# Keys and values made by rows from x in two parts, queries moved behind the context, w1 and w2 staged in SBUF

## The reference

```python
Q = x @ wq.T;  K = x @ wk.T;  V = x @ wv.T               # 4096 x 64 each
energy  = einsum('nd,ne->de', K, V)                      # 64 x 64
context = Q @ energy * sqrt(3 / 64)
x = layernorm(x + context @ wo.T)
h = silu((x @ w1.T) * s1) * ((x @ w2.T) * s2)            # 4096 x 1024
h = gelu((h @ h1.T) * s_h1);  h = gelu((h @ h2.T) * s_h2)
out = layernorm(x + (h @ w3.T) * s3)
```

## Time and profile before

| | us |
|---|---|
| median of 3 runs (lowest, highest) | 647.01 (646.89, 647.16) |
| the profiled execution | 647.28 |
| its span, first to last instruction | 645.5 |
| PE busy | 635.5 (98%) |
| DVE busy | 491.1 (76%) |
| ACT busy | 411.0 (64%) |
| POOL busy | 280.6 (43%) |

### The profile page before, as it was taken

One profiled execution on the slowest core, in us unless ns is written; L12 is line 12 of the kernel. 1 busy time (PEld: TensorE's weight loads), 2 busy tenths in 40 slices (PEclk: granted clock), 3 DMA queues, 4 the chain that ended last, 5 costly groups with the idle time before them and its releaser, 6 DMA issues.

```text
span 645.5 us, 9171 instructions
## 1 busy us (share of the span) xinstructions
PE 635.5 (98%) x3147; PEld 531.1 (82%) x3148; DVE 491.1 (76%) x722; ACT 411.0 (64%) x697; POOL 280.6 (43%) x225
## 2 busy tenths in 40 slices
PE   8989999999999999999999999999999999999996
PEld 6768887888789888888889888888889888888896
DVE  5687799989565996789665898698754899488477
ACT  6579688868672566558661757656763466666655
POOL 0376999492001762096000564078000367069025
PEclk9999999999999999999999999999999999999999
DMA  8999889953310056434330036734330015534301
GB/s 342 391 367 401 321 333 354 378 205 130 133 67 0 2 163 229 162 131 147 129 116 1 1 97 191 251 118 159 130 131 1 0 20 188 184 131 144 118 1 67
DMA packets 24370, 103.89 MB, mean 161 GB/s; under 512 B 2224, under 2 KB 3312, under 8 KB 16496
## 3 DMA queue, kind: packets, MB, share of 16 engines
q1 hardware_dynamic: 24032, 102.98, 45.1%
q10 hardware_dynamic: 288, 0.26, 0.1%
HBM read 87.51 MB, written 23.07 MB: 171 GB/s over the span
## 4 chain that ended last, share of the span: by engine, by line
PE 97%; DVE 1%; issue 0%; POOL 0%; POOLq 0%; ACT 0%; DVEq 0%
PE ps L1395 63%; PE ps L1338 18%; PE ps L1464 8%; PE ps L1487 1%; PE ps L1270 1%; PE ps L1204 1%; PE ps L1232 1%; PE ps L1258 1%; PE ps L1246 1%; PE ps L1220 1%; PE ps L1252 0%; PE ps L1239 0%; DVE st L1125 0%; DVE xr L1132 0%; POOL rstd L512 0%
## 5 line engine op out<-in xcount | busy, mean ns | idle before, releaser
L1395 PE MATMUL ps<-R,ring 128*128 128x512 f32 x1792 | 410.2, 390 | 0.2 <-issue 0.2
L1395 PEld LDWEIGHTS ps<-R,ring 128*128 128x128 f32 x1792 | 335.2, 188 | 69.9 <-issue 0.6
L984 DVE TENSOR_TENSOR R<-quarter,R 128x512 fp32r<-128x512 f32 x284 | 262.0, 946 | 58.8 <-ACT R L709 58.5
L709 ACT CAST R<-quarter 128x512 fp32r<-128x512 f32 x284 | 173.2, 616 | 30.0 <-POOL quarter L540 12.0
L1338 PE MATMUL ps<-x1T,w 128*128 128x512 f32 x512 | 119.1, 391 | 0.6 <-issue 0.5
L755 ACT ACTIVATE quarter<-U,sc 128x512 f32<-128x512 f32 x96 | 69.5, 724 | 73.7 <-DVE U L1011 28.3
L1338 PEld LDWEIGHTS ps<-x1T,w 128*128 128x128 f32 x512 | 95.4, 188 | 21.9 <-ACT quarter L755 0.9
L530 POOL TENSOR_TENSOR quarter<-quarter,quarter 128x512 f32<-128x512 f32 x32 | 50.4, 1576 | 95.0 <-ACT quarter L755 88.3
L673 ACT ACTIVATE sg<-ps,sc 128x512 f32<-128x512 f32 x64 | 44.2, 690 | 63.6 <-PE ps L1338 63.5
L481 POOL TENSOR_TENSOR ve<-mv,eps 128x4 f32<-128x4 f32 x14 | 5.6, 403 | 180.4 <-DVE mv L961 180.4
L725 ACT COPY U<-ps 128x512 f32<-128x512 f32 x96 | 56.2, 585 | 28.7 <-PE ps L1395 28.5
(11 more groups left out here) (97 smaller groups left out, 389.1 us busy)
## 6 DMA issues: line engine op xcount, KB each, us to landing
ring<-combos SPq DMA_DIRECT2D x56, 1024.0 KB, 4.9
combos<-unit SPq DMA_DIRECT2D x8, 1024.0 KB, 8.5
unit<-in_h1T SPq DMA_DIRECT2D x4, 1024.0 KB, 14.6
xr<-in_x_rows SPq DMA_DIRECT2D x8, 512.0 KB, 5.1
unit<-in_h2T SPq DMA_DIRECT2D x4, 1024.0 KB, 8.7
xT<-in_xT SPq DMA_DIRECT2D x7, 512.0 KB, 7.7
out<-xr SPq DMA_DIRECT2D x7, 512.0 KB, 3.0
w<-w_dram SPq DMA_DIRECT2D x3, 1024.0 KB, 9.3
```

What stands on the lines that cost most here:

```text
L709: nc.scalar.copy(R[slot_of(p, u)][:, 0, c, :], quarter[operand_home(p, u)][:, c, :]).then_inc(hi_done, 1)
L984: nc.vector.tensor_tensor(r[:, 1, c, :], quarter[operand_home(p, u)][:, c, :], r[:, 0, c, :].bitcast(f32), ALU.subtract).then_inc(lo_done, 1)
L1395: last = nc.tensor.matmul(ps[:, bank + j, :], w, view(R[slot_of(p, u)][:, part, k, :]), start=n in (0, 1, 5) and k == 0 and part == 0, sto ...
```

## The change

- Keys and values of blocks 2 to 7 are made by rows from the two parts: `kv_of_parts` has, for each of 4 tiles, 4 fp32r matmuls with a 128x128 piece of `xhi` or `xlo` stationary and `wkvr` (128 columns) moving. The transposed products, the turning and their copies go. VectorE copies blocks 0 to 2, ScalarE 3 to 7, into four buffers in place of two.
- All eight blocks keep their own `xhi` (the last four where the ring is loaded later), so rounding waits for no queries. The low part of block 1 moves from VectorE to the head of GpSimd's queue.
- Queries: only block 0's stand ahead of keys and values. Of block 1, two pieces stand ahead of T1; the other 26 stand behind it. The 5 warm-up products go; the banks change.
- ScalarE's order changes: `bits_of_w12(0)` ahead of T1's rounding, `bits_of_whole(1)` behind `hi_of_transposed(0, 6)`, `bits_of_whole(2)` and `(3)` at j = 2 and 3 of the first silu loop, in place of j = 0 and 5, with the sums of unit 0 at j = 0 and 1.
- w1 and w2 are loaded into SBUF where units 3 and 4 come later (`w12_stage`), looked at there and copied within SBUF. Loads of units 3 and 4 wait for that. `load_unit(4)` is issued behind the stores of the queries, `load_ring(5)` ahead of `load_rows_late`.

The diff, cut to its core:

```diff
--- before.py
+++ after.py
@@ -49,13 +49,11 @@
-Q_BETWEEN = 4
+KV_DVE = 3
...
-Q_BANK = (4, 5, 6, 7, 5, 4, 5, 3)
+Q_BANK = (4, 5, 6, 7, 4, 6, 7, 4)
...
-WARM_MIDDLE = 5
@@ -152,10 +151,11 @@
-        kvT = [over(f"kvT{i}", q_at + 8192 + 1024 + 2048 * i, [P, BLK]) for i in range(2)]
...
-        xhi = [over(f"xhi{i}", x1T_at + 4096 * i, [P, EC, BLK], f32r) for i in range(4)]
+        xhi = [over(f"xhi{f}", x1T_at + 4096 * f if f < 4 else ring_at + 4096 * (f - 4), [P, EC, BLK], f32r) for f in range(NB)]
...
+        w12_stage = over("w12_stage", u_at, [P, 2 * EC * HID])
@@ -310,14 +310,14 @@
-            def relay_w12(i):
+            def stage_w12(i):
                 at = i * EC * HID
-                sp.dma_start(w12_dram[:, at:at + EC * HID], (w1_in, w2_in)[i]).then_inc(w12_relayed[i], 16)
+                sp.dma_start(w12_stage[:, at:at + EC * HID], (w1_in, w2_in)[i]).then_inc(w12_staged[i], 16)
...
                 at = i * EC * HID
-                sp.wait_ge(w12_relayed[i], 16)
-                sp.dma_start(w12[:, at:at + EC * HID].bitcast(f32), w12_dram[:, at:at + EC * HID]).then_inc(w12_in[i], 16)
+                sp.wait_ge(w12_staged[i], 16)
+                sp.dma_start(w12[:, at:at + EC * HID].bitcast(f32), w12_stage[:, at:at + EC * HID]).then_inc(w12_in[i], 16)
@@ -327,6 +327,9 @@
                     sp.wait_ge(l1_tile, 2 * HC * (i - 5))
+                if 3 <= i <= 4:
+                    sp.wait_ge(w12_in[i - 3], 16)
+                    sp.wait_ge(bits_done, n_bits("w12", i - 3))
                 src = sources[i // KH].rearrange("p (h i n) -> p h i n", h=2, i=KH)[:, :, i % KH, :]
@@ -371,16 +374,16 @@
             store_unit(0)
+            relay_hidden(0, 0)
             store_q(4)
-            relay_hidden(0, 0)
-            load_unit(4)
-            store_unit(1)
             store_q(5)
...
             store_q(7)
-            store_unit(2)
+            load_unit(4)
+            store_unit(1)
             load_ring(0)
             relay_hidden(0, 1)
+            store_unit(2)
             store_unit(3)
@@ -391,10 +394,10 @@
             relay_hidden(1, 0)
+            load_ring(5)
             load_rows_late(3)
...
             relay_hidden(1, 1)
-            load_ring(5)
             store_unit(5)
@@ -551,6 +554,10 @@
+            pool.wait_ge(kv_ready, 2)
+            pool.wait_ge(xhi_done, 2)
+            nc.gpsimd.tensor_tensor(tiles_of(xlo[1]), tiles_of(xT[1]), xhi[1].bitcast(f32).rearrange("p c (t n) -> p c t n", t=TPB),
+                                    ALU.subtract).then_inc(second_xlo, 1)
@@ -596,10 +603,12 @@
-            def copy_kvt(f):
...
-                act.wait_ge(kvt_ready, f - 1)
-                nc.scalar.copy(kvT[f % 2][:, :], ps[:, KV_BANK[f], :]).then_inc(kvt_out, 1)
+            def copy_kv(f):
...
+                act.wait_ge(kv_ready, f + 1)
+                if f >= 4:
+                    act.wait_ge(et_ready, f - 3)
+                nc.scalar.copy(kv[f % 4][:, :], ps[:, KV_BANK[f], :]).then_inc(later_kv_out, 1)
@@ -608,13 +617,11 @@
-                if f >= 4:
-                    act.wait_ge(q_ready, f - 3)
-                nc.scalar.copy(xhi[f % 4].rearrange("p c (t n) -> p c t n", t=TPB), tiles_of(xT[f])).then_inc(xhi_done, 1)
+                nc.scalar.copy(xhi[f].rearrange("p c (t n) -> p c t n", t=TPB), tiles_of(xT[f])).then_inc(xhi_done, 1)
...
-                act.wait_ge(w12_in[i], 16)
-                bits(low_halves(w12[:, i * EC * HID:(i + 1) * EC * HID]), 0, i)
+                act.wait_ge(w12_staged[i], 16)
+                bits(low_halves(w12_stage[:, i * EC * HID:(i + 1) * EC * HID]), 0, i)
@@ -826,44 +833,42 @@
                 high_x(f)
-            copy_kvt(2)
             hi_of_q(0)
             high_x(5)
-            copy_kvt(3)
-            hi_of_q(1)
             high_x(6)
-            copy_kvt(4)
-            raw_q(2)
+            copy_kv(3)
             high_x(7)
-            raw_q(3)
-            for f in range(5, NB):
-                copy_kvt(f)
+            copy_kv(4)
+            copy_kv(5)
             bits_of_whole(0)
-            raw_q(4)
+            copy_kv(6)
+            copy_kv(7)
+            bits_of_w12(0)
             act.wait_ge(t1_ready, 1)
             nc.scalar.activation(T1s[:, 0, :], ps[:, 3, 0:E], ACT.Copy, scale=CTX_SCALE).then_inc(t1_hi, 1)
-            for i in range(2):
-                bits_of_w12(i)
-            bits_of_whole(1)
+            hi_of_q(1)
+            bits_of_w12(1)
+            raw_q(2)
+            raw_q(3)
+            raw_q(4)
             for q in range(ACT_TILES[0]):
...
             raw_q(6)
+            raw_q(7)
             hi_of_transposed(0, 6)
-            raw_q(7)
+            bits_of_whole(1)
             act.wait_ge(cst_in, 16 * NCST)
...
                 silu(0, j, A)
-                if j == 0:
-                    bits_of_whole(2)
+                if j <= 1:
+                    bits_of_sums(0, range(j, j + 1))
                 if 2 <= j <= 3:
-                    bits_of_sums(0, range(j - 2, j - 1))
+                    bits_of_whole(j)
                 if j == TR1_AFTER:
...
                     hi(0, 0, j - KH)
-                if j == 5:
-                    bits_of_whole(3)
             for j in range(HC):
@@ -1091,24 +1096,22 @@
             nc.vector.memset(zeros[:, :], 0.0).then_inc(zeros_made, 1)
-            for f in range(NB):
+            def copy_kv(f):
                 dve.wait_ge(kv_ready, f + 1)
-                if f >= 2:
-                    dve.wait_ge(et_ready, f - 1)
-                nc.vector.tensor_copy(kv[f % 2][:, :], ps[:, KV_BANK[f], :]).then_inc(kv_out, 1)
-                if f == 0:
-                    low_x(0)
-                    flag_out(0)
-                elif f == 1:
-                    low_x(2)
-                    low_x(1)
-                    low_x(3)
-                    low_x(4)
-                    lo_of_q(0)
-                elif f <= 4:
-                    if f == 4:
-                        lo_of_q(1)
-                    low_x(f + 3)
+                nc.vector.tensor_copy(kv[f][:, :], ps[:, KV_BANK[f], :]).then_inc(kv_out, 1)
+
+            copy_kv(0)
+            low_x(0)
+            flag_out(0)
+            copy_kv(1)
+            low_x(2)
+            low_x(3)
+            low_x(4)
+            copy_kv(2)
+            lo_of_q(0)
+            low_x(5)
+            low_x(6)
+            low_x(7)
             dve.wait_ge(et_ready, NB)
@@ -1144,6 +1147,7 @@
+            lo_of_q(1)
@@ -1197,10 +1201,10 @@
-                            pe.wait_ge(*((qlo_done, 2), (qlo_done, 1), (q_raw, 3), (tile_sum[0], TPB))[b - 4])
+                            pe.wait_ge(*((qlo_done, 1), (q_raw, 1), (q_raw, 2), (q_raw, 3))[b - 4])
...
-                        pe.wait_ge(xlo_done, n_xlo(b))
-                    x = xhi[b % 4][:, c, :] if part == 0 else tiles_of(xlo[b])[:, c, :, :]
+                        pe.wait_ge(*((second_xlo, 1) if b == 1 else (xlo_done, n_xlo(b))))
+                    x = xhi[b][:, c, :] if part == 0 else tiles_of(xlo[b])[:, c, :, :]
@@ -1221,28 +1225,27 @@
-            def kv_transposed(f, view):
...
-                if f > 2:
-                    pe.wait_ge(kv_out, f - 2)
-                for part in range(2):
-                    pe.wait_ge(*((xhi_done, f + 1) if part == 0 else (xlo_done, n_xlo(f))))
-                    for c in range(EC):
-                        x = xhi[f % 4][:, c, :] if part == 0 else tiles_of(xlo[f])[:, c, :, :]
-                        last = nc.tensor.matmul(ps[:, KV_BANK[f], :], wkvr[:, c, :] if view is exact else wkv[:, c, :], view(x),
-                                                start=part == 0 and c == 0, stop=part == 1 and c == 1)
-                last.then_inc(kvt_ready, 1)
...
-            def kv_turned(f):
-                pe.wait_ge(kvt_out, f - 1)
+            def kv_of_parts(f, view):
...
+                if f >= 3:
+                    pe.wait_ge(*kv_copied(f - 3))
+                pe.wait_ge(xhi_done, f + 1)
+                pe.wait_ge(xlo_done, n_xlo(f))
...
-                    last = nc.tensor.transpose(ps[:, KV_BANK[f], q * P:(q + 1) * P], kvT[f % 2][:, q * P:(q + 1) * P], ident[:, :])
+                    for part in range(2):
+                        for c in range(EC):
+                            x = xhi[f][:, c, q * P:(q + 1) * P] if part == 0 else tiles_of(xlo[f])[:, c, q, :]
+                            last = nc.tensor.matmul(ps[:, KV_BANK[f], q * P:(q + 1) * P], view(x), wkvr[:, c, :] if view is exact else wkv[:, c, :],
+                                                    start=part == 0 and c == 0, stop=part == 1 and c == 1)
...
+            def kv_copied(f):
+                return (kv_out, f + 1) if f < KV_DVE else (later_kv_out, f - KV_DVE + 1)
...
-                pe.wait_ge(kv_out, f + 1)
+                pe.wait_ge(*kv_copied(f))
...
-                    k, v = kv[f % 2][:, q * P:q * P + D], kv[f % 2][:, q * P + D:(q + 1) * P]
```

(57 more changed lines are left out.)

3 lines of the change are left out of this document (removed).

## The result

The changed kernel is slower. In the first round the median over both groups was 657.7 against 647.05 before; the lower group stands to the kernel before as 1.0075 (95% interval 1.0056 to 1.0095), in the second round as 1.0068 (1.0053 to 1.0082).

The account below looks back on a forecast made before the run. TensorE was taken to bound the kernel, with 97% of the last-ending chain. The terms -0.7 - 0.1 + 3.1 - 0.2 = +2.1 us took the profiled 647.28 to 649.4, median 649.1; range 645.7 to 651.8.

Parts of the forecast that it names:

- The sum: Whole kernel: all terms together +2.1 us, so 649.4 for the profiled execution and 649.1 for the median.
- Part 1: TensorE's stretch ahead of product T1: 16.8 us against 17.45, so T1 starts 0.7 us earlier.
- c: Spacing of fp32r matmuls of 128 columns ahead of T1: taken as 0.115 us, within 0.107 to 0.128.
- The engines that feed this stretch keep up: Ahead of T1: VectorE, ScalarE and GpSimd deliver in time despite moved work; cost taken as 0.
- Part 2: From T1 to the first w1 product: 14 more query pieces are hidden, change -0.1 us.
- Rival (c), the clock: Wait at block 1's transposes: TensorE's clock falls there, adding 1.6 to 2.5 us; chance 12%.
- Part 3: Block 1's transposes: its deviation, queued on GpSimd behind combinations that start later, makes TensorE wait 3.1 us.
- Part 4: Transfers: copying w1 and w2 within SBUF and later unit loads cost 0; an earlier ring load gives -0.2 us.
- The hole at ring 5: TensorE's hole of 0.21 us ahead of 106.66: issuing `load_ring(5)` earlier removes it, -0.2 us.

Follow-up runs that it names:

- e1: Changed kernel with block 1's low part moved from GpSimd back to VectorE; median 650.62 us, ratio 1.0054.
- e3: Changed kernel with block 1's low part back on VectorE and block 1's deviation ahead of unit 2 in GpSimd's queue; median 646.13 us, ratio 0.9973.
- e10: e7 with 12 wide warm-up products put between the narrow ones; 650.78 to 653.75 us, ratio 1.0092.
- b5: Kernel before with only block 1's low part moved to the head of GpSimd's queue; median 649.21 us, ratio 1.0025.
- b6: Kernel before with only ScalarE's looks put in the new order; median 652.26 us, ratio 1.0077.
- e4: Changed kernel with six warm-up products filling the hole ahead of the first narrow products; median 651.88 us, ratio 1.0078.
- e2: Changed kernel with block 1's deviation ahead of unit 2 in GpSimd's queue; seven executions 646.45 to 648.38 us (ratio 0.9997), three 657.5 to 658.6.
- e7: e3 with its first narrow products made to wait for VectorE's low part of block 4; 647.68, 658.05, 658.65 and 658.96 us.
- b8: Kernel before with its first 128x512 products of keys and values made to wait for block 4's low part; median 653.17 us, ratio 1.0091.
- a0: Changed kernel measured again, unedited, in a second round; four executions 649.38 to 652.77 us, two 662.95 and 664.15.

## Why the prediction was wrong

- **The sum** came out for one execution in eleven, the one whose clock holds: +2.1 forecast, a span of 647.5 against 645.5, and 649.38 against the 649.4 I had put on the profiled execution. In part this is luck, as the next point shows.
- **Part 1.** The stretch from energy(1) to T1 took 16.82 in that execution (10.99 to 27.81), as my 16.8, but by two errors that cancel. Without the hole it takes 15.93 (e1, e3), 0.9 less than I had: the six blocks 11.3 against 11.84 and the seven energies 4.0 against 4.27. The hole of 0.84, which I had put at nothing, made up for it. T1 was 1.0 earlier and not 0.7 because that execution also came to this place earlier (block 0's query pieces began at 9.91, before at 10.29).
- **c** was 0.112 us (14 steps of two products between the starts 14.19 and 17.32 in e10), against my 0.115. Of the two rules of the Trainium skill's "TensorE: Matmul & The Clock Gate" that I had weighed, LDWEIGHTS with 107 ns is near this, and Back-to-back issue gap with 81 ns is not.
- **"The engines that feed this stretch keep up"** is the first step that failed, a wait that I put at nothing. I gave GpSimd the low part of block 1 as free because GpSimd was idle, and did not ask what runs on VectorE beside it. It stretched VectorE's low part of block 2 from 1.2 to 2.9 us and opened a hole of 0.84 in one trace and 1.37 in the other. I had even used the same effect in part 2, to explain 2.19 against 1.38. The Trainium skill ("SBUF — State Buffer", Who interferes with whom) says that a VectorE instruction with two SBUF inputs and a GpSimd instruction that reads SBUF lock each other out. e1 and b5 agree with it: VectorE's three low parts took 3.49 without GpSimd's subtraction beside them and 5.24 with it.
- **Rival (c), the clock**, is the second, and the larger. I looked for a fall only in the wait at block 1, gave it 12%, and priced it at 1.6 to 2.5. It was seen there in three of five traces that have the wait (the upper group's, e1, b6; not in the lower group's nor e4) and cost 1.4 to 1.6. And I did not put it at the front at all, where it costs 11: that is how far the medians of the two groups lie apart in the changed kernel, in e2 and in e7. What I had not asked is how the clock comes back. Behind the hole it fell, and under the narrow products it stayed down for some 20 us (the upper group's trace and e7), while b8 had it back after 3.4. Which property of the narrow stream does that (its 128 columns, a weight load for every product) was not tested.
- **Part 2:** from T1 to the first w1 product 9.99, before 9.87: +0.1 instead of -0.1. The 14 more pieces are hidden, as forecast.
- **Part 3** held step by step. After T1's start: `combine(1)` at +11.37 (forecast +11.3), unit 2's first addition at +17.19 (+17.2), the deviation at +19.82 (+19.8), VectorE's tiles at +21.16 (+21.15), the wait 2.93 (3.1). b6 shows that the order of ScalarE's looks alone makes it, e2 that GpSimd's order alone removes it.
- **Part 4:** the copies within SBUF took 6.2 us each, not 9.3, and were hidden as before. The hole at ring 5 went, but by 157 us holes of 0.24 behind a flag's sum and 0.17 ahead of transposes had taken its place, so -0.2 was 0.

## What to carry to other kernels

Before giving work to an idle engine, ask what the other engines that read SBUF do at that moment, and which waits on others stand behind it in the same queue: one subtraction here held up TensorE, and two tiny operations behind six large ones cost 2.9 us. Don't put a long run of narrow matmuls behind a place where TensorE may stand still. If it must be, fill the place (e4) or put wide products between (e10); each had four executions and no long one. A sum that meets the measured time is not yet right: here a hole and too high a price for the products hid each other. And work that can move behind the point where another engine sets the pace is worth moving (3.2 us of queries were hidden), while the form of the products ahead of it has to be priced by itself.

## What the runs showed of the hardware

- fp32r matmuls with 128 moving columns and a new weight each start 0.112 us apart at 2.4 GHz and 0.2135 at 1.2 GHz; with 512 columns it is 0.23 at 2.4 GHz. So a narrow one does a quarter of the columns in half the time.
- Under such a stream, with single energies of 64 columns between, a fallen clock stayed at 0.50 for 19.6 us (the upper group's trace) and 21.4 us (e7) without a hole. In b8 it was back after 3.4 us of mostly 128x512 products, in e7 during three energies in a row, in the upper group's trace only behind them. TensorE was busy for all of these stretches by the profile, so the busy share does not tell what the clock will do.
- Without a hole the same narrow stream kept its clock: none of the 14 executions of e1 and e3 was long, against 10 of 25 in the three kernels with the hole and nothing wide behind it (4 of 11 in the changed kernel, 3 of 10 in e2, 3 of 4 in e7). What decides between the executions of one kernel was not shown. Of the five traces with the hole and narrow products behind it, the two with the longest holes (1.37 and 1.41) have the fall and those with 0.84, 0.84 (a0, e2) and 1.27 (e10) don't, which is too few to tell.
- Two subtractions of SBUF tensors, 128x1024 each, on VectorE and GpSimd at once: VectorE's took 2.9 us in place of 1.2, beside GpSimd's of 2.37.
- A transfer of 1 MB within SBUF landed in 6.2 us (issued at 20.7) where one from DRAM took 9.3 (issued at 18.3). The traffic beside them differed, so this is no clean comparison.
